# Transposes of an adaptive FFN kernel moved from the DMA queue to TensorE, and the queue reordered

## The chip, the cores and the metric

The kernel runs on one core of one Trainium2 chip. The metric is the device time of one execution in microseconds (us). Before the change it is 73.77 us, the median of three runs (73.26 to 75.43).

## What is computed

x has 2 x 1024 rows of 256 values. Each batch has its own 256x256 matrix, made from 30 ranks, and the result goes through a two-layer network with quantised weights and activations:

```
U = (mu @ W_dec + b_dec).reshape(B, 257, 30)
param = einsum('bik,kj->bij', U, V)                  # V: 30 x 256
y = einsum('bsd,bde->bse', x, param[:, :-1]) + param[:, -1][:, None]
quant_act(v): scale = 127 / max(|v| over the row), then round(v * scale) / scale
quant_weight(w): s = mean(|w|), then clip(round(w / s), -1, 1) * s
h = gelu(quant_act(y) @ quant_weight(w1).T)          # 1024 wide
out = x + quant_act(h) @ quant_weight(w2).T
```

## The kernel before

The 2048 rows are 16 tiles of 128 rows, and two tiles are a pair (0 to 7). A tile goes through these steps. z is the product of x with U (30 wide), made for four tiles at once (`product_z`); y is z times V, made for a pair (`product_y`, line 427). VectorE takes the maxima of y and their reciprocals; ScalarE rounds y by adding a large constant (`quantise_y`, line 573), so that the integer stands in the low 16 bits of an fp32 word. The quantised y has to be transposed before the first product (`product_1`, line 445), whose result ScalarE turns into h by a gelu (line 595). VectorE takes the maxima of h for a pair at once (line 698), GpSimd quantises a tile of h into fp16 with an offset of 1152 added (`quantise_h`, line 366), h is transposed, and the second product (`product_2`, line 462) gives a tile of the output. The offset is taken out by one more product per tile with the row sums of w2 (line 472; the sums are made by `offset_sums`). VectorE scales the result and adds x (`output`, line 740), and SyncE stores a pair.

There are two ways to transpose. For pairs 0 and 1 of y TensorE transposes the low halves and VectorE copies them out of PSUM (`transpose_yq` in the TensorE block, `copy_yqt`, line 691). From pair 2 on GpSimd narrows y to bf16 (`narrow_y`, line 338) and SyncE issues a DMA transpose (line 260); the h of tiles 0 to 13 go by DMA transpose too (line 267). The h of the last two tiles are transposed by TensorE in halves (line 485) and copied out by ScalarE and VectorE (lines 631, 638, 793, 797). Of tile 15 VectorE quantises one half (line 788) and ScalarE the other (line 634).

The order on each engine is written out by hand, and each engine runs its list in order. TensorE's main loop (lines 544 to 550) runs, for p from 3, the first products of pair p, y of pair p + 2 between them, and the second products of pair p - 3. VectorE's (line 770) runs the maxima of h of pair p, an output, the maxima of y of pair p + 3, the scales of both, an output. GpSimd's (line 375) runs tile 2p of h, the small product for the scales, the narrowing of pair p + 3, tile 2p + 1. SyncE's list after the loads is

```
transpose_yq(AHEAD - 1)
for p in range(PAIRS):
    transpose_hq(2 * p)
    if p < Y_PAIRS: transpose_yq(p + AHEAD)
    transpose_hq(2 * p + 1)
    if p >= LAG // 2: store(2 * p - LAG, 2 * p - LAG + 2)
```

with AHEAD = 3, PAIRS = 7, Y_PAIRS = 5 and LAG = 6. The transposed h have six buffers, the quantised h four (a tile waits until the one four before it has been transposed), the h three pairs. Seven products of zeros, `keep_warm(7, ps_o)` (line 537), stand before the product of tile 4.

Of the kernel before, what the change touches and what calls it, by code (L numbers as in the profile page):

```python
# [6 lines left out]
FP16 = mybir.dt.float16  # L7
# [21 lines left out]
def adaln_ffn(nc, x, x_tr, small, w_dec, w1_tr, w2_tr, out):  # L29
# [23 lines left out]
    SINGLE = 2 * PAIRS  # L53

# [4 lines left out]
    with ctx:  # L59
# [79 lines left out]
        def blocks(bank, n, dt=BF16):  # L139
# [11 lines left out]
        ps_yqt = [blocks(ps_o, DC), blocks(ps_z, DC), blocks(ps_o, 2 * DC)]  # L151
# [5 lines left out]
        ps_hqt = {NT - 2: [blocks(ps_y[:, half, :], HC // 2, FP16) for half in range(2)],  # L157
                  NT - 1: [blocks(ps_h[0][:, half, :], HC // 2, FP16) for half in range(2)]}
# [64 lines left out]
        hqt14_done = sem("tile14_hqt_half_done")  # L223
        hqt14_copied = [sem(f"tile14_hqt_copied{n}") for n in range(2)]
        last_hq = [sem(f"last_hq_ready{n}") for n in range(2)]
        last_hqt = sem("last_hqt_half_done")
        last_hqt_copied = [sem(f"last_hqt_copied{n}") for n in range(2)]
# [6 lines left out]
        def yqt_count(p):  # L234

            return 16 * (p // 2)
# [11 lines left out]
        def _(sp):  # L248
# [9 lines left out]
            def transpose_yq(p):  # L258
                sp.wait_ge(yqh_ready, p - 1)
                sp.dma_start_transpose(yq_t[:, p, :, :, :].rearrange("p t c q -> p (t c) q"),  # L260
                                       yq_h[p % 2][:, :, :].rearrange("p t c -> p (t c)")).then_inc(yqt_landed[p % 2], 16)
# [45 lines left out]
        def _(pool):  # L307
# [26 lines left out]
            def narrow_y(p):  # L334
                pool.wait_ge(yq_ready, 2 * p + 2)
                if p >= 4:
# [45 lines left out]
            for n in range(SINGLE, NT):  # L382
                scale_h(n)

        @block.tensor
        def _(pe):
            def keep_warm(n, bank=ps_idle):
                for _ in range(n):
                    nc.tensor.matmul(bank, warm_h[:, 0:P], warm_h[:, :], start=True, stop=True)  # L389
# [17 lines left out]
            def offset_sums():  # L407
                for n in range(2):
# [28 lines left out]
            def transpose_yq(n):  # L437

                pe.wait_ge(yq_ready, (1, 2, 4)[n])
                i0, i1 = ((0, 1), (1, 2), (0, 2))[n]  # L440
                for c in range(DC * i0, DC * i1):
                    last = nc.tensor.transpose(ps_yqt[n][:, c - DC * i0, :], yq_low[n // 2][:, c * P:(c + 1) * P], ident_h[:, :])
                last.then_inc(yqt_done, 1)

            def product_1(n):
# [3 lines left out]
                elif n >= 4 and n % 2 == 0:  # L449
# [12 lines left out]
            def product_2(n):  # L462
# [9 lines left out]
                nc.tensor.matmul(o_of[n], offsets[:, :], w2_off[:, :], start=True, stop=False)  # L472
                if n < NT - 2:
                    pe.wait_ge(hqt_landed[k], 16 * (n // LAG + 1))
                for t in range(HC):
                    if n >= NT - 2 and t % (HC // 2) == 0:
                        pe.wait_ge((hqt14_copied, last_hqt_copied)[n - NT + 2][t // (HC // 2)], 1)
                    last = nc.tensor.matmul(o_of[n], hq_t[k][:, t, :], w2_t[:, t, :], start=False, stop=(t == HC - 1))  # L478
                last.then_inc(mm2_done, 1)

            def transpose_hq(n, half):

                for t in range(HC // 2):
                    c = half * HC // 2 + t
                    last = nc.tensor.transpose(ps_hqt[n][half][:, t, :], hq_h[n % NB][:, c * P:(c + 1) * P], ident_f[:, :])
                last.then_inc((hqt14_done, last_hqt)[n - NT + 2], 1)
# [64 lines left out]
            product_2(NT - 6)  # L551
            product_2(NT - 5)
            pe.wait_ge(hq_ready, NT - 1)
            for half in range(2):
                transpose_hq(NT - 2, half)
            pe.wait_ge(last_hq[0], 1)
# [289 lines left out]
```

## Time and profile before

| | |
|---|---|
| median of three runs | 73.77 us (73.26 to 75.43) |
| the profiled execution | 73.63 us, its span 71.8 us |
| busy, share of the span | TensorE 85%, VectorE 64%, ScalarE 46%, GpSimd 41% |
| HBM read / written | 10.47 MB / 2.10 MB |
| chain of waits, by engine | GpSimd 23%, DMA 19%, TensorE 19%, issue 13%, VectorE 9%, SyncE 8% |

The span is the time from the program's first instruction to its last; the execution's time has something more around it. Busy time counts an engine's own instructions; an engine can be idle and still be the one that the others wait for. In the views PE is TensorE, PEld its weight loads, DVE VectorE, ACT ScalarE, POOL GpSimd and SPq what SyncE issues. The loads end at about 27 us, and the change begins behind them.

### The profile page before, as it was taken

The numbers are of one execution on the slowest core, as the hardware profiler recorded it, in microseconds if no ns is written. First come the engines' busy times: TensorE is split into PE (matmuls) and PEld (weight loads), VectorE is DVE, ScalarE is ACT, GpSimd is POOL, SyncE is SP. The second block draws the span as 40 slices with busy tenths as digits, with TensorE's granted clock in tenths as the row PEclk, the third lists the DMA queues.
The fourth block names the chain that finished last, engine by engine and source line by source line (L and its number), as shares of the span: only waits on it lengthen the run. The fifth ranks groups of instructions, "written<-read, shape, count | busy, mean of one in ns | idle before, by whom it ended". The sixth has DMA issues, their size and how long they took to land.

```text
span 71.8 us, 1271 instructions
## 1 busy us (share of the span) xinstructions
PE 60.8 (85%) x452; PEld 31.6 (44%) x452; DVE 45.9 (64%) x92; ACT 33.3 (46%) x47; POOL 29.5 (41%) x48
## 2 busy tenths in 40 slices
PE   2999999988986999959909999999994698889930
PEld 1315232223323534414603664847662266669820
DVE  2002437644367848999585589798988907998440
ACT  3406009200382979947843766947592074044100
POOL 5500000000001088989596276593969484520000
PEclk9999999999999999999999999999999999999999
DMA  0899999999999995030969979658894699999352
GB/s 7 229 383 415 422 413 410 410 387 409 413 433 415 420 415 246 14 73 10 73 145 176 189 136 187 127 110 170 171 200 100 133 265 175 275 187 365 117 219 73
DMA packets 22086, 17.10 MB, mean 238 GB/s; under 512 B 18496, under 2 KB 18880, under 8 KB 21696
## 3 DMA queue, kind: packets, MB, share of 16 engines
q1 hardware_dynamic: 21936, 16.78, 81.7%
q10 hardware_dynamic: 144, 0.24, 1.6%
q8 instruction: 3, 0.05, 0.4%
q14 instruction: 3, 0.02, 0.1%
HBM read 10.47 MB, written 2.10 MB: 175 GB/s over the span
## 4 chain that ended last, share of the span: by engine, by line
POOL 23%; DMA 19%; PE 19%; issue 13%; DVE 9%; SPq 8%; ACT 4%; POOLq 0%; ACTq 0%
POOL hq_h L366 16%; DMA w_dec_all<-in_w_dec_dram 16%; PE ps_h L457 5%; SPq L250 5%; POOL yq_h L338 4%; PE ps_o L478 4%; DMA yq_t<-yq_h 4%; DVE h_max L716 3%; POOL w_t L351 3%; PE ps_z L478 2%; PE ps_z L422 2%; DVE o_sb L740 2%; ACT w_dec_all L595 2%; ACT y_q L584 1%; ACT w_r L571 1%
## 5 line engine op out<-in xcount | busy, mean ns | idle before, releaser
L366 POOL TENSOR_SCALAR hq_h<-w_dec_all,pair_rcp 128x1024 f16<-128x1024 f32 x14 | 15.7, 1119 | 7.8 <-DVE pair_rcp L712 7.2
L457 PE MATMUL ps_h<-w_t,yq_t 128*128 128x512 bf16 x64 | 15.8, 380 | 3.2 <-DMA yq_t<-yq_h 3.2
L698 DVE TENSOR_REDUCE pair_max<-w_dec_all 128x2 f32<-128x2048 f32 x7 | 15.9, 2273 | 0.0
L595 ACT ACTIVATE w_dec_all<-ps_h,pair_c 128x1024 f32<-128x1024 f32 x10 | 10.9, 1112 | 10.2 <-PE ps_h L457 10.2
L389 PE MATMUL ps_h<-warm_h 128*128 128x512 bf16 x39 | 13.3, 462 | 1.3 <-POOL warm_h L308 1.3
L457 PEld LDWEIGHTS ps_h<-w_t,yq_t 128*128 128x128 bf16 x64 | 5.6, 98 | 10.5 <-DMA yq_t<-yq_h 4.3
L478 PE MATMUL ps_z<-w_t,hq_t 128*128 128x256 f16 x64 | 8.3, 273 | 1.0 <-DMA hq_t<-hq_h 1.0
L324 POOL TENSOR_TENSOR c<-y_inv,s 128x2 f32<-128x2 f32 x3 | 0.6, 194 | 20.3 <-DVE y_inv L686 20.3
L478 PE MATMUL ps_o<-w_t,hq_t 128*128 128x256 f16 x64 | 8.3, 273 | 0.5 <-DMA hq_t<-hq_h 0.5
L389 PEld LDWEIGHTS ps_h<-warm_h 128*128 128x128 bf16 x39 | 3.8, 119 | 7.9 <-issue 6.1
L478 PEld LDWEIGHTS ps_z<-w_t,hq_t 128*128 128x128 f16 x64 | 6.1, 98 | 2.1 <-DMA hq_t<-hq_h 1.4
L478 PEld LDWEIGHTS ps_o<-w_t,hq_t 128*128 128x128 f16 x64 | 6.1, 98 | 2.0 <-DMA hq_t<-hq_h 0.8
L567 ACT ACTIVATE w_abs<-w_sb 128x1024 f32<-128x1024 f32 (+1 forms) x3 | 2.7, 914 | 9.1 <-DMA w_sb<-in_w_tr_dram 9.0
L595 ACT ACTIVATE w_dec_all<-ps_h,c 128x1024 f32<-128x1024 f32 x6 | 6.5, 1114 | 0.9 <-PE ps_h L457 0.9
L740 DVE SCALAR_TENSOR_TENSOR o_sb<-ps_o,pair_c,x_sb 128x256 f32<-128x256 f32 x7 | 3.4, 483 | 4.4 <-PE ps_o L478 4.4
L646 DVE TENSOR_REDUCE w_sum<-w_sb 128x1 f32<-128x1024 f32 (+1 forms) x2 | 1.9, 948 | 5.4 <-DMA w_sb<-in_w_tr_dram 5.4
L571 ACT ACTIVATE w_r<-w_sb,s_rcp 128x1024 int16<-128x1024 f32 x3 | 3.3, 1141 | 4.1 <-DVE s_rcp L656 4.1
L434 PE MATMUL ps_y<-small_sb,z_t 30*128 30x256 f32 x28 | 4.9, 425 | 0.2 <-DVE z_t L677 0.2
L584 ACT ACTIVATE y_q<-ps_y,pair_rcp 128x256 f32<-128x256 f32 x10 | 4.2, 471 | 1.0 <-DVE pair_rcp L712 1.0
L703 DVE TENSOR_REDUCE pair_max<-ps_y 128x2 f32<-128x512 f32 x5 | 3.4, 685 | 1.4 <-PE ps_y L434 1.4
L338 POOL TENSOR_SCALAR yq_h<-y_q 128x512 bf16<-128x512 f32 x6 | 3.7, 617 | 0.7 <-ACT y_q L584 0.7
L740 DVE SCALAR_TENSOR_TENSOR o_sb<-ps_z,pair_c,x_sb 128x256 f32<-128x256 f32 x7 | 3.3, 477 | 0.7 <-PE ps_z L478 0.7
(88 smaller groups left out, 68.3 us busy)
## 6 DMA issues: line engine op xcount, KB each, us to landing
w_sb<-in_w_tr_dram SPq DMA_DIRECT2D x4, 512.0 KB, 8.8
x_sb<-in_x_dram SPq DMA_DIRECT2D x2, 1024.0 KB, 18.9
out_dram<-o_sb SPq DMA_DIRECT2D x7, 256.0 KB, 2.7
w_dec_all<-in_w_dec_dram SPq DMA_DIRECT2D x3, 512.0 KB, 7.5
w_dec_all<-in_w_dec_dram SPq DMA_DIRECT2D x3, 448.0 KB, 8.2
x_t<-in_x_tr_dram SPq DMA_DIRECT2D x1, 1024.0 KB, 16.5
w_dec_all<-in_w_dec_dram SPq DMA_DIRECT2D x1, 576.0 KB, 10.5
x_t<-in_x_tr_dram SPq DMA_DIRECT2D x2, 256.0 KB, 11.0
```

Source lines behind the costliest of these rows:

```text
L250: sp.dma_start(w_dec_all[:, starts[n]:starts[n + 1]], w_dec[:, starts[n]:starts[n + 1]]).then_inc(s_wdec[n], 16)
L338: pool.tensor_scalar(yq_h[p % 2][:, :, :].rearrange("p t c -> p (t c)"), y_q[p % 2][:, :, :].rearrange("p t c -> p (t c)"), 1.0, -MAGIC, A ...
L366: pool.tensor_scalar(hq_h[n % NB][:, :], h_tile(n), scale, H_OFFSET, ALU.mult, ALU.add).then_inc(hq_ready, 1)
L389: nc.tensor.matmul(bank, warm_h[:, 0:P], warm_h[:, :], start=True, stop=True)
L434: last = nc.tensor.matmul(y_of[p][:, i, 0:D], z_t[p // 2][r:r + K, :], v_sb[r:r + K, :], start=True, stop=True)
L457: last = nc.tensor.matmul(ps_h[k][:, half, :], yq_t[:, p, n % 2, c, :], w1_t[:, c, half * HALF:(half + 1) * HALF], start=(c == 0), stop=(c ...
L478: last = nc.tensor.matmul(o_of[n], hq_t[k][:, t, :], w2_t[:, t, :], start=False, stop=(t == HC - 1))
L571: nc.scalar.activation(dst, src, ACT.Copy, scale=scale).then_inc(done, 1)
L584: nc.scalar.activation(y_q[p % 2][:, i, :], y_of[p][:, i, 0:D], ACT.Copy, bias=MAGIC, scale=scale).then_inc(yq_ready, 1)
L595: nc.scalar.activation(h_tile(n), ps_h[n % 2][:, :, :].rearrange("p a n -> p (a n)"), ACT.Gelu, scale=c1_of(n)).then_inc(gelu_done, 1)
L698: nc.vector.tensor_reduce(pair_max[:, p, 2:4], h_pair[p % NH], AXX, ALU.max, apply_absolute_value=True).then_inc(pair_max_ready, 1)
L740: nc.vector.scalar_tensor_tensor(o_sb[p % NO][:, i, :], o_of[n], c2_of(n), x_sb[:, b, t, :], ALU.mult, ALU.add).then_inc(out_ready, 1)
```

## The change

Three things change. Pairs 2 and 3 of y are transposed by TensorE like pairs 0 and 1, but ScalarE copies them out; GpSimd narrows only pairs 4 to 7. The seven products of zeros go, and the row sums of w2 are made behind the product of tile 6. SyncE's list has the store first, then y, then both tiles of h. The h of tiles 12 and 13 join those of 14 and 15: TensorE transposes them in halves, and ScalarE and VectorE copy them out and take the offset off in the copy, so these four tiles have no product with the row sums. GpSimd takes over ScalarE's half of tile 15.

```
 SyncE
-            transpose_yq(AHEAD - 1)
             for p in range(PAIRS):
-                transpose_hq(2 * p)
-                if p < Y_PAIRS:
-                    transpose_yq(p + AHEAD)
-                transpose_hq(2 * p + 1)
                 if p >= LAG // 2:
                     store(2 * p - LAG, 2 * p - LAG + 2)
+                if 1 <= p < Y_PAIRS:
+                    transpose_yq(p + AHEAD)
+                if 2 * p < LATE:                      # LATE = NT - 4
+                    transpose_hq(2 * p)
+                    transpose_hq(2 * p + 1)
 GpSimd
-            narrow_y(AHEAD - 1)
...
-                if p < Y_PAIRS:
+                if 1 <= p < Y_PAIRS:
                     narrow_y(p + AHEAD)
...
-            for n in range(SINGLE, NT):
-                scale_h(n)
+            scale_h(NT - 2)
+            pool.wait_ge(h_rcp_ready, NT - SINGLE)
+            pool.wait_ge(hqt_landed[(NT - 1 - NB) % LAG], 16 * ((NT - 1 - NB) // LAG + 1))
+            pool.tensor_scalar(hq_h[(NT - 1) % NB][:, HALF:], h_tile(NT - 1)[:, HALF:], h_rcp[:, NT - 1:NT], H_OFFSET,
+                               ALU.mult, ALU.add).then_inc(last_hq[1], 1)
+            scale_h(NT - 1)
 TensorE
             product_z(2)
+            transpose_yq(3)
             product_y(3)
-            keep_warm(7, ps_o[:, :])
             product_1(4)
             product_1(5)
+            transpose_yq(4)
             product_y(4)
-            offset_sums()
             pe.wait_ge(z_copied, 3)
             product_z(3)
             for p in range(LAG // 2, NP):
                 product_1(2 * p)
+                if p == LAG // 2:
+                    offset_sums()
...
-            product_2(NT - 6)
-            product_2(NT - 5)
-            (transposes of tiles 14 and 15 between the second products 10 to 15)
+            for n in range(LATE, NT):
+                for half in range(2):
+                    transpose_hq(n, half)
+                product_2(n - 2)
+            product_2(NT - 2)
+            product_2(NT - 1)
 ScalarE
             for p in range(AHEAD, NP):
                 gelu(2 * p - 4)
-                gelu(2 * p - 3)
-                if p == AHEAD + 1:
+                if p - 1 < 4:
+                    copy_yqt(p - 1)
+                if p == AHEAD + 2:
                     ...                                # the copy of the row sums
+                gelu(2 * p - 3)
                 quantise_y(p)
...
+            def copy_yqt(p):
+                act.wait_ge(yqt_done, p + 2)
+                nc.scalar.activation(yq_t[:, p, ...], ps_yqt[p + 1].bitcast(I16), ACT.Copy,
+                                     bias=-OFFSET).then_inc(yqt_copied, 1)
+            for n, half in ((LATE, 0), (LATE, 1), (LATE + 1, 0), (LATE + 1, 1), (LATE + 2, 0), (LATE + 3, 1)):
+                act.wait_ge(late_hqt, 2 * (n - LATE) + half + 1)
+                act.wait_ge(mm2_done, n - LAG + 1)
+                part = slice(half * HC // 2, (half + 1) * HC // 2)
+                nc.scalar.activation(hq_t[n % LAG][:, part, :], ps_hqt[n][half], ACT.Copy,
+                                     bias=-H_OFFSET).then_inc(late_copied[n][half], 1)
 VectorE, after its half of tile 15
             output(NT - 6)
             output(NT - 5)
+            copy_late(NT - 2, 1)                       # a tensor_scalar that adds -H_OFFSET
+            copy_late(NT - 1, 0)
             for n in range(NT - 4, NT):
                 output(n)
```

The late tiles' transposes go to the banks of y and of the first products, each with a wait for its last reader.

## Rows read from the trace of the kernel before

**Rows 1.** The page, costliest groups: count | busy us, mean ns | idle us before, releaser.
```profile
L366 POOL TENSOR_SCALAR hq_h<-w_dec_all,pair_rcp 128x1024 f16<-128x1024 f32 x14 | 15.7, 1119 | 7.8 <-DVE pair_rcp L712 7.2
...
L698 DVE TENSOR_REDUCE pair_max<-w_dec_all 128x2 f32<-128x2048 f32 x7 | 15.9, 2273 | 0.0
...
L324 POOL TENSOR_TENSOR c<-y_inv,s 128x2 f32<-128x2 f32 x3 | 0.6, 194 | 20.3 <-DVE y_inv L686 20.3
...
L584 ACT ACTIVATE y_q<-ps_y,pair_rcp 128x256 f32<-128x256 f32 x10 | 4.2, 471 | 1.0 <-DVE pair_rcp L712 1.0
L703 DVE TENSOR_REDUCE pair_max<-ps_y 128x2 f32<-128x512 f32 x5 | 3.4, 685 | 1.4 <-PE ps_y L434 1.4
```

**Rows 2.** The page: granted clock in 40 slices; an instruction queue's packets.
```profile
PEclk9999999999999999999999999999999999999999
...
q8 instruction: 3, 0.05, 0.4%
```

**Rows 3.** The chain of waits around 54 us: start, length, what.
```profile
54.19 2.58 DMA yq_t<-yq_h
```

**Rows 4.** The timeline, 28 to 34 us: start, length, what [idle before <- releaser].
```profile
28.62 2.12 ACT L595 ACTIVATE w_dec_all<-ps_h,c 128x1024 f32<-128x1024 f32 x2
28.82 0.62 POOL L338 TENSOR_SCALAR yq_h<-y_q 128x512 bf16<-128x512 f32 x1 [0.40 <-ACT y_q L584]
...
29.41 2.04 POOL L351 TENSOR_SCALAR w_t<-w_r 128x1024 f16<-128x1024 int16 x2
...
29.51 1.69 PE L389 MATMUL ps_o<-warm_h 128*128 128x512 bf16 x7
...
30.61 0.87 DVE L709 TENSOR_SCALAR pair_inv<-pair_max 128x4 f32<-128x4 f32 x1
...
31.84 2.27 DVE L698 TENSOR_REDUCE pair_max<-w_dec_all 128x2 f32<-128x2048 f32 x1
```

**Rows 5.** The timeline, 35 to 47 us.
```profile
35.31 0.17 DVE L709 TENSOR_SCALAR pair_inv<-pair_max 128x4 f32<-128x4 f32 x1
...
37.87 1.04 PE L457 MATMUL ps_h<-w_t,yq_t 128*128 128x512 bf16 x4 [1.78 <-DMA yq_t<-yq_h]
...
42.31 1.03 PE L457 MATMUL ps_h<-w_t,yq_t 128*128 128x512 bf16 x4
...
43.27 0.70 PE L434 MATMUL ps_y<-small_sb,z_t 30*128 30x256 f32 x4
...
46.74 1.03 PE L457 MATMUL ps_h<-w_t,yq_t 128*128 128x512 bf16 x4
```

**Rows 6.** SyncE's timeline: a store's issue.
```profile
50.81 0.58 SPq L274 DMA_DIRECT2D out_dram<-o_sb  x1
```

**Rows 7.** By tile, h and y: issues in ns and landing in us, min/median/max.
```profile
L267 SPq DMA_TRANSPOSE hq_t<-hq_h x14: 1233/1302/2653, 32.9 to 62.3; - x14
...
DMA to landing us min/median/max: 3.1/3.4/5.6
...
L260 SPq DMA_TRANSPOSE yq_t<-yq_h x6: 1262/1278/2325, 29.5 to 54.2; - x6
...
DMA to landing us min/median/max: 2.5/2.5/3.6
```

**Rows 8.** The timeline, 55 to 70 us.
```profile
55.14 1.05 PE L478 MATMUL ps_z<-w_t,hq_t 128*128 128x256 f16 x8 [0.99 <-DMA hq_t<-hq_h]
...
56.82 1.90 PE L457 MATMUL ps_h<-w_t,yq_t 128*128 128x512 bf16 x8 [0.63 <-DMA yq_t<-yq_h]
...
63.35 0.61 PE L485 MATMUL ps_y<-ident_f,hq_h 128*128 128x128 f16 x8
...
63.77 0.60 ACT L631 ACTIVATE hq_t<-ps_y 128x512 f16<-128x512 f16 x1 [3.76 <-PE ps_y L485]
...
64.75 1.04 PE L478 MATMUL ps_o<-w_t,hq_t 128*128 128x256 f16 x8
...
68.99 0.48 DVE L740 SCALAR_TENSOR_TENSOR o_sb<-ps_z,c,x_sb 128x256 f32<-128x256 f32 x1 [0.50 <-PE ps_z L478]
```

More of the change, by code:

```diff
@@ L222, in adaln_ffn @@
         out_ready = sem("out_ready")
-        hqt14_done = sem("tile14_hqt_half_done")
-        hqt14_copied = [sem(f"tile14_hqt_copied{n}") for n in range(2)]
+        late_hqt = sem("late_hqt_half_done")
+        late_copied = {n: [sem(f"late_hqt{n}_copied{half}") for half in range(2)] for n in range(LATE, NT)}
         last_hq = [sem(f"last_hq_ready{n}") for n in range(2)]
-        last_hqt = sem("last_hqt_half_done")
-        last_hqt_copied = [sem(f"last_hqt_copied{n}") for n in range(2)]
         store_done = [sem(f"store_done{k}") for k in range(NO)]
@@ L437, in transpose_yq @@
             def transpose_yq(n):
-                pe.wait_ge(yq_ready, (1, 2, 4)[n])
-                i0, i1 = ((0, 1), (1, 2), (0, 2))[n]
+                p, i0, i1 = YQT_PARTS[n]
+                pe.wait_ge(yq_ready, 2 * p + i1)
+                if n > 2:
+                    pe.wait_ge(yqt_copied, n)
                 for c in range(DC * i0, DC * i1):
-                    last = nc.tensor.transpose(ps_yqt[n][:, c - DC * i0, :], yq_low[n // 2][:, c * P:(c + 1) * P], ident_h[:, :])
+                    last = nc.tensor.transpose(ps_yqt[n][:, c - DC * i0, :], yq_low[p % 2][:, c * P:(c + 1) * P], ident_h[:, :])
                 last.then_inc(yqt_done, 1)
@@ L448, in product_1 @@
                     pe.wait_ge(yqt_copied, n + 1)
-                elif n >= 4 and n % 2 == 0:
+                elif n in (4, 6):
+                    pe.wait_ge(yqt_copied, p + 2)
+                elif n >= 8 and n % 2 == 0:
                     pe.wait_ge(yqt_landed[p % 2], yqt_count(p))
@@ L471, in product_2 @@
                     pe.wait_ge(out_ready, n - 1)
-                nc.tensor.matmul(o_of[n], offsets[:, :], w2_off[:, :], start=True, stop=False)
-                if n < NT - 2:
+                if n < LATE:
+                    nc.tensor.matmul(o_of[n], offsets[:, :], w2_off[:, :], start=True, stop=False)
                     pe.wait_ge(hqt_landed[k], 16 * (n // LAG + 1))
                 for t in range(HC):
-                    if n >= NT - 2 and t % (HC // 2) == 0:
-                        pe.wait_ge((hqt14_copied, last_hqt_copied)[n - NT + 2][t // (HC // 2)], 1)
-                    last = nc.tensor.matmul(o_of[n], hq_t[k][:, t, :], w2_t[:, t, :], start=False, stop=(t == HC - 1))
+                    if n >= LATE and t % (HC // 2) == 0:
+                        pe.wait_ge(late_copied[n][t // (HC // 2)], 1)
+                    last = nc.tensor.matmul(o_of[n], hq_t[k][:, t, :], w2_t[:, t, :], start=(n >= LATE and t == 0), stop=(t == HC - 1))
                 last.then_inc(mm2_done, 1)
             def transpose_hq(n, half):
+                if n < NT - 1:
+                    pe.wait_ge(hq_ready, n + 1)
+                else:
+                    pe.wait_ge(last_hq[half], 1)
+                if n == LATE:
+                    pe.wait_ge(yq_ready, NT)
+                elif n == LATE + 2:
+                    pe.wait_ge(late_copied[LATE][half], 1)
+                else:
+                    pe.wait_ge(gelu_done, NT - 1 if n == LATE + 1 else NT)
                 for t in range(HC // 2):
@@ L485, in transpose_hq @@
                     last = nc.tensor.transpose(ps_hqt[n][half][:, t, :], hq_h[n % NB][:, c * P:(c + 1) * P], ident_f[:, :])
-                last.then_inc((hqt14_done, last_hqt)[n - NT + 2], 1)
+                last.then_inc(late_hqt, 1)
             pe.wait_ge(s_warmh, 1)
@@ L550, in _ @@
                 product_2(2 * p - LAG + 1)
-            product_2(NT - 6)
-            product_2(NT - 5)
[L553 to L556, printed above, removed]
-            transpose_hq(NT - 1, 0)
-            product_2(NT - 4)
-            pe.wait_ge(last_hq[1], 1)
-            transpose_hq(NT - 1, 1)
-            for n in range(NT - 3, NT):
-                product_2(n)
+            for n in range(LATE, NT):
[4 more added lines that the diff above has]
+            product_2(NT - 1)
         @block.scalar
@@ L741, in output, with copy_late @@
                                                ALU.mult, ALU.add).then_inc(out_ready, 1)
+            def copy_late(n, half):
+                dve.wait_ge(late_hqt, 2 * (n - LATE) + half + 1)
+                dve.wait_ge(mm2_done, n - LAG + 1)
+                part = slice(half * HC // 2, (half + 1) * HC // 2)
+                nc.vector.tensor_scalar(hq_t[n % LAG][:, part, :], ps_hqt[n][half], -H_OFFSET, None,
+                                        ALU.add).then_inc(late_copied[n][half], 1)
             nc.vector.memset(ps_z[:, :], 0.0).then_inc(s_psz, 1)
```

42 lines of the change are left out of this document (15 added, 27 removed).

## The prediction

> **What bounds the kernel now.** I began with the page. Its costliest groups [rows 1] show three streams that are nearly level over the second half of the span: VectorE with seven maxima of h of 2.27 us, GpSimd with fourteen quantisations of 1.12 us, and ScalarE with its gelus. None is full by itself, so the question is which wait ends last. The granted clock is 9 tenths or more in every slice [rows 2], the 2.4 GHz level, so the clock takes nothing now.
>
> The timeline of the middle [rows 5] gives the rhythm: the product of tile 8 starts at 42.31 and that of tile 10 at 46.74, 4.43 us for a pair in which TensorE never waits. VectorE's work in the same pair is 2.27 + 0.68 [rows 1] + two outputs of 0.48 [rows 8] + 0.4 for a scaling, a reciprocal of its size and the hops between them [rows 5], that is 4.3 at most. So here TensorE is the bound with VectorE close behind.
>
> The lost time is at three places, and each waits for a transposed tile. Tile 6's first product waits 1.78 us for pair 3 of y [rows 5]. Tile 7's second product waits 0.99 us for its h, and right behind it tile 14's first product 0.63 us for pair 7 of y [rows 8]. The chain of waits runs through that last one: its transfer takes 2.58 us from its issue at 54.19 [rows 3]. Two rows say why it was late. SyncE needs about 1.3 us to issue any transpose, and two issues, one of h and one of y, took 2.65 and 2.33 us instead [rows 7]; one transfer of h took 5.6 us to land against a median of 3.4 [rows 7]. I call these two events holds. One delayed pair 3, the other tile 7's h and pair 7. Without the second one tile 14 could have started where TensorE was free: 51.17, where tile 12's product ran (4.43 behind tile 10's 46.74), plus two first products of 0.87 and two second ones of 0.98, 54.9 instead of 56.82.
>
> From tile 14 to the last output at 68.99 + 0.48 = 69.47 the kernel is one ladder of VectorE and TensorE steps of 12.65 us.
>
> **Part 1, pairs 2 and 3 of y through TensorE.** Removed from GpSimd: the narrowing of pair 2, 0.62 us, which runs just ahead of the two clips of w2, 2.04 us, that end at 31.45 [rows 4]. VectorE's tiny scaling began at 30.61 and took 0.87 us, against 0.17 in another pair [rows 5]: it ended when the clips ended. With the clips 0.4 to 0.6 earlier (they then wait for GpSimd's own scale of y) they end near 30.5, before VectorE asks. The reciprocal of pair 0 comes at about 31.1, 0.6 earlier. The Trainium skill (GPSIMD Engine Reference, Specifications) says that GpSimd shares its SBUF interfaces with VectorE when that is in a two-port mode; the row agrees, and it is a warning for part 3.
>
> Added to ScalarE: two copies of 128x512 out of PSUM. The nearest row is the copy of half a tile of h, same shape, 0.60 us [rows 8]; a gelu of twice the columns, 1.06, bounds it above [rows 4], and 0.47 for half the columns bounds it below (line 584) [rows 1]. I take 0.6. The first stands before the gelu of tile 3, so that one ends at 31.3, not 30.74, and the maximum of pair 1, which began at 31.84 because of the scaling, begins at 31.4. Added to TensorE: eight transposes of 128 columns, eight of the same shape in fp16 take 0.61 [rows 8]; they stand where seven warming products of 1.69 us stood [rows 4], so they cost nothing; without that cover they would be 0.3 each.
>
> Now step by step. VectorE: 31.4 + 2.27 + 0.68 + 0.4 gives the reciprocals of pair 1 at 34.8. GpSimd then quantises (1.12), multiplies its scales (0.2 by the small product of line 324) [rows 1] and narrows pair 4 (0.62) [rows 4], 0.1 with the hops: 36.85. Its transfer, 2.5 us [rows 7], lands at 39.4. TensorE: the gelu of tile 4 ends at 33.2, ScalarE's second copy at 33.8, so tile 6's product starts at 34.0 instead of 37.87. Behind its 0.87 (eight in 1.90 are two tiles) come the row sums of w2 (eight of 256 columns, 1.0) [rows 8], y (0.70) [rows 5], tile 7 (0.87) and two second products (1.96), which with the hops fill up to 39.4. Both sides meet there: tile 8 starts at 39.4 instead of 42.31, **2.9 us earlier**. A copy of 1.06 instead of 0.6 would take up to 0.5 of this back.
>
> **Part 2, the order of the queue.** Two h transposes of each pair now stand behind its y, and a store of 0.58 [rows 6] ahead of it. The store asks for an output that VectorE makes before the reciprocals that this y needs, so it adds its issue and no wait. The h that are pushed back have three pairs until they are read. TensorE keeps its 4.43: tile 12 at 48.3, tile 14 possible at 48.3 + 3.7 = 52.0. But SyncE becomes the tighter queue: from pair 4's issue at 36.85 to pair 7's there are three rounds of 1.28 + 2 x 1.30 + gaps of 0.15 = 4.03 and two stores of 0.65, so pair 7 is issued at 50.2 and lands at 52.7. That is 56.82 - 52.7 = **4.1 earlier if nothing holds the queue**.
>
> The two holds were not made by this order. What I can see beside them is that the page counts three packets of 16 KB in an instruction queue which take 0.4% of sixteen engines' span, 1.5 us each [rows 2], and a hold is 1.05 to 1.35 us longer than a normal issue [rows 7]. My guess, which no view of this profile shows, is that these packets refill TensorE's program at fixed places of it and that a transpose in flight then is held. TensorE's program is hardly longer ahead of tile 13 (14 instructions of the warming products go, 16 of the transposes come). Then the first falls on h transposes with slack, and the second near 49 to 51, where transposes of h 7 and y 7 follow each other without a gap. I take it to come again, at 1.2 us: tile 14 at 53.9, **2.9 earlier**. The Trainium skill, Runtime: NRT & Kernel Launch, Instruction fetch mechanics, calls the crossing of a 16 KiB boundary mostly hidden; by that nothing is held in the new order, which is the first rival.
>
> **Part 3, the last four tiles.** Added to TensorE: sixteen transposes, 2 x 0.61 = 1.22 [rows 8]; removed: four products with the offsets, of 256 columns and so 0.11 apiece by the eight in 1.04, 0.44 in all. Added to ScalarE: four more copies, 2.4 us, in a stretch where it waited 3.76 us before its one; its half of tile 15's quantisation goes to GpSimd (0.62, by the narrowing of the same shape [rows 4]). The ladder from tile 14: VectorE's output 8, two maxima, two scales, output 9, its half of tile 15 and output 10 are the same steps as before and lead to tile 12's second product 7.9 us behind tile 14's start (64.75 less 56.82) [rows 8]. Then 0.87 + transposes 0.53 + 3 x 0.87 + drain 0.17 + output 0.48 = 4.66, 12.5 in all against 12.65: **0.15 less**. The extra transposes of tiles 12 and 13 fall into the wait for output 10. If that cover is gone they cost 1.2 - 0.44 = 0.8. GpSimd and VectorE now quantise their halves of tile 15 side by side; if they exclude each other as at 30.61, one of them is 0.5 to 0.6 late. Tile 15's transposes come some 0.8 later than that, so I take 0, and keep 0.6 for the range.
>
> Nothing in the tail now needs h transposes 12 to 15 from the queue, which frees 5.2 us of SyncE (4 x 1.30); that was not on the chain, and I count it at zero. The last stores are the same.
>
> **Sum.** The profiled execution took 73.63 us with a span of 71.8; it lies 0.14 under the median of 73.77. 2.9 + 0.15 = 3.1 off gives 70.5 from the profiled execution and 70.7 from the median; I take **70.5**.
>
> **Rivals.**
> No hold on the path: 4.1 + 0.15 off, **69.4**. For it: the hold needs a transpose just then, and there are six fewer of them. Against: the queue is denser around pair 7.
> The queue or ScalarE takes more back: issue times of 1.4 instead of 1.3 over nine issues ahead of pair 7 (0.9), or copies at their upper bound, with a hold: **71.7**. Against: SyncE's median is firm.
> The tail becomes the bound: TensorE's added 0.8, the halves of tile 15 in turn 0.6, and the start of tile 14 held twice (1.2): 70.5 + 2.6 = **73.1**, no difference. It decides if output 10 no longer is what tile 12's product waits for.
> Slower: TensorE's clock. The warming products go, and TensorE waits from 29.9 to 30.3 for ScalarE's copy and 0.1 to 0.2 for the gelu of tile 3 at 31.3. If the granted clock fell to 1.2 GHz there, eight products that take 1.90 [rows 8] would take 3.8; TensorE has some 9 us of work from 30.3 up to tile 8 at 39.4, so it is slower than before by over 2% once the low level lasts over 4.6 us: **79** if it lasts all of it. Against: a wait of 1.78 us in rows 5 did not lower it, and the new ones are shorter.
> That the change does not do what it says is no separate case: pair 3 of y and the h of tiles 12 to 15 no longer pass the queue at all.
>
> **Chances.** Forecast 0.45, no hold 0.25, queue or copies 0.17, tail 0.10, clock 0.03. A measurement can tell 2% from no change, that is 72.3 and below or 75.2 and above. So faster 0.88 (a part of the third case lies above 72.3, a part of the tail below), same 0.10, slower 0.02. The range goes from 68.9 (no hold, and issues at their shortest, 1.23 to 1.26, nine times 0.05) to 72.1 (the third case with half a microsecond of tail).
>
> **What would show it.** The profile after should have tile 6's product near 34.0, tile 8's at 39.4, tile 14's between 52.7 and 54; VectorE's scaling of pair 0 at 0.17 us; a period of 4.4 between; SyncE issuing with no gap from pair 4 on; 12.5 us from tile 14 to the end. The prediction is wrong if tile 14 still waits for y by more than 2 us, if ScalarE's gelus start late behind its copies, or if the tail is longer than 13 us.

## The result, and the profile after

| | median, us | lowest to highest | executions |
|---|---|---|---|
| before | 74.60 | 73.26 to 76.03 | 4 |
| changed | 71.15 | 70.77 to 72.01 | 4 |

The ratio of changed to before is 0.968, 95% interval 0.958 to 0.979: faster, by 3.2%. A second measurement of the same two kernels (the first run below) gave 0.969 (0.961 to 0.976). The ratios leave disturbed executions out and the medians don't (before's 75.43 and 76.03 raise its median), so the two medians are further apart, 4.6%, than the ratio says. The profiled execution took 70.77 us with a span of 68.9, against 73.63 and 71.8: 2.86 us less.

The core's granted clock, the packets of the instruction queue and two groups of the page, for [rows 1, 2]. A quantisation of h costs what it did (1.12 us), and so does a maximum (2.28 us), so the gain is in waits and in the products of zeros that filled one.

```profile
core 0: 68.9 us, clock 1.000
q8 instruction: 3, 0.05, 0.3%
L367 POOL TENSOR_SCALAR hq_h<-w_dec_all,pair_rcp 128x1024 f16<-128x1024 f32 x14 | 15.7, 1122 | 8.4 <-DVE pair_rcp L729 6.1
L486 PE MATMUL ps_o<-w_t,hq_t 128*128 128x256 f16 x64 | 8.3, 273 | 2.1 <-DMA hq_t<-hq_h 1.8
```

The timeline from 29 to 40 us, which answers [rows 4] and the head of [rows 5]: start, length, what, idle before. The scaling of pair 0 (line 726) takes 0.17 where it took 0.87. Tile 6's product starts 0.17 ahead of the line at 34.08 (one of its four records is missing), and pair 4 of y is issued at 36.84.

```profile
29.78 0.61 ACT L614 ACTIVATE yq_t<-ps_o 128x512 bf16<-128x512 int16 x1
30.77 0.17 DVE L726 TENSOR_SCALAR pair_inv<-pair_max 128x4 f32<-128x4 f32 x1
...
31.43 2.29 DVE L715 TENSOR_REDUCE pair_max<-w_dec_all 128x2 f32<-128x2048 f32 x1
...
34.08 0.81 PE L465 MATMUL ps_h<-w_t,yq_t 128*128 128x512 bf16 x3 [0.16 <-issue]
...
36.84 1.19 SPq L261 DMA_TRANSPOSE yq_t<-yq_h  x1
...
39.28 1.04 PE L465 MATMUL ps_h<-w_t,yq_t 128*128 128x512 bf16 x4
```

The same view from 44 to 55 us, which answers [rows 5, 6] and the first two lines of [rows 8]. SyncE issues with no gap. Its h transposes issued at 46.82 land late; tile 6's second product (51.85) waits 1.62 us for them, GpSimd (51.96) waits 1.64 us for the same transfer, because the buffer it wants to write is still being read, and tile 14's product waits for pair 7 of y. Its first record is missing: it began at 54.06, so of the 0.40 us in its line only some 0.2 are a wait (0.15 in the profile of the swap below, where no record is missing).

```profile
44.85 0.58 SPq L275 DMA_DIRECT2D out_dram<-o_sb  x1
45.48 1.23 SPq L261 DMA_TRANSPOSE yq_t<-yq_h  x1
46.82 2.62 SPq L268 DMA_TRANSPOSE hq_t<-hq_h  x2
...
50.12 1.72 SPq L261 DMA_TRANSPOSE yq_t<-yq_h  x1
51.85 1.05 PE L486 MATMUL ps_o<-w_t,hq_t 128*128 128x256 f16 x8 [1.62 <-DMA hq_t<-hq_h]
51.96 1.12 POOL L367 TENSOR_SCALAR hq_h<-w_dec_all,pair_rcp 128x1024 f16<-128x1024 f32 x1 [1.64 <-DMA hq_t<-hq_h]
54.28 1.67 PE L465 MATMUL ps_h<-w_t,yq_t 128*128 128x512 bf16 x7 [0.40 <-DMA yq_t<-yq_h]
```

By tile, h and then y, as in [rows 7]: issues in ns, landing in us, each as minimum, median and maximum.

```profile
L268 SPq DMA_TRANSPOSE hq_t<-hq_h x12: 1237/1297/2307, 32.4 to 56.7; - x12
DMA to landing us min/median/max: 3.1/3.3/5.0
L261 SPq DMA_TRANSPOSE yq_t<-yq_h x4: 1190/1254/1724, 36.8 to 50.1; - x4
DMA to landing us min/median/max: 2.4/2.6/3.9
```

The chain that ended last, from 46 us to tile 10's second product; its columns are start, length, what. [Rows 3] had a transfer of y there. Now the chain has two of h. The first holds the buffer that GpSimd wants for tile 10 (51.96). The chain then goes on through tile 11's quantisation (53.45), which ends as SyncE comes free, but that is a coincidence.

```profile
46.82 4.98 DMA hq_t<-hq_h
51.96 0.71 POOL hq_h L367
...
53.45 1.12 POOL hq_h L367
54.62 0.57 SPq L275
55.28 3.31 DMA hq_t<-hq_h
58.64 1.05 PE ps_o L486 x8
```

Tile 10's h was ready at 51.96 + 1.12 = 53.08 and still was not issued before 55.28. SyncE's own timeline shows why: behind pair 7 (50.12) it issues the h of tiles 8 and 9, a store, and then tile 10's h, without a gap. So it is the full queue that sets tile 10's product, not GpSimd.

```profile
51.94 2.63 SPq L268 DMA_TRANSPOSE hq_t<-hq_h  x2
54.62 0.57 SPq L275 DMA_DIRECT2D out_dram<-o_sb  x1
55.28 2.66 SPq L268 DMA_TRANSPOSE hq_t<-hq_h  x2
```

The tail, against the rest of [rows 8]. From tile 14's start (about 54.06) to the end of the last output (66.49) it takes 12.43 us; it took 12.65.

```profile
60.92 0.49 DVE L812 TENSOR_SCALAR hq_h<-w_dec_all,h_rcp 128x512 f16<-128x512 f32 x1
60.99 0.98 POOL L385 TENSOR_SCALAR hq_h<-w_dec_all,h_rcp 128x512 f16<-128x512 f32 x1 [0.52 <-DVE h_rcp L741]
61.33 0.48 DVE L757 SCALAR_TENSOR_TENSOR o_sb<-ps_o,pair_c,x_sb 128x256 f32<-128x256 f32 x1
61.86 1.05 PE L486 MATMUL ps_o<-w_t,hq_t 128*128 128x256 f16 x8 [0.30 <-DVE o_sb L757]
...
66.01 0.48 DVE L757 SCALAR_TENSOR_TENSOR o_sb<-ps_z,c,x_sb 128x256 f32<-128x256 f32 x1 [0.39 <-PE ps_z L486]
```

### The profile page after: what moved, and what is told of

It is laid out like the page before. It is cut to its first block, busy times and chain, and to the rows that moved or that the text cites. A ratio compares the mean times of both kernels' runs of the same rounds, so it can differ in the third digit from the quotient of the medians.

```text
span 68.9 us, 1306 instructions
## 1 busy us (share of the span) xinstructions
PE 58.7 (85%) x459; PEld 31.7 (46%) x465; DVE 45.1 (65%) x92; ACT 35.6 (52%) x52; POOL 29.4 (43%) x47
## 4 chain that ended last, share of the span: by engine, by line
DMA 28%; PE 18%; DVE 14%; SPq 12%; POOL 9%; ACT 7%; issue 7%; POOLq 0%; DVEq 0%
DMA w_dec_all<-in_w_dec_dram 16%; DMA hq_t<-hq_h 12%; POOL hq_h L367 7%; DVE pair_max L715 7%; SPq L251 5%; PE ps_o L486 4%; PE ps_z L486 4%; ACT w_dec_all L609 4%; PE ps_h L465 2%; PE ps_z L427 2%; SPq L261 2%; DVE pair_max L720 2%; SPq L275 2%; ACT y_q L598 1%; SPq L268 1%
## 5 line engine op out<-in xcount | busy, mean ns | idle before, releaser
L465 PE MATMUL ps_h<-w_t,yq_t 128*128 128x512 bf16 x60 | 15.1, 380 | 1.1 <-ACT yq_t L614 0.5
L393 PE MATMUL ps_h<-warm_h 128*128 128x512 bf16 x37 | 12.4, 450 | 1.5 <-POOL warm_h L309 1.3
L348 POOL TENSOR_SCALAR w_r<-w_sb,s_rcp 128x1024 int16<-128x1024 f32 x1 | 2.8, 2848 | 1.9 <-DVE s_rcp L673 1.9
```

The costliest lines, as they stand in the source:

```text
L393: nc.tensor.matmul(ps_idle, warm_h[:, 0:P], warm_h[:, :], start=True, stop=True)
L465: last = nc.tensor.matmul(ps_h[k][:, half, :], yq_t[:, p, n % 2, c, :], w1_t[:, c, half * HALF:(half + 1) * HALF], start=(c == 0), stop=(c ...
```

## The experiments

**The changed kernel again**, unaltered.

> The changed kernel unaltered, for a narrower interval. Theory (the start is 2.9 us earlier, the hold comes again, the tail costs 0.1): profiled execution again 70.8 +- 0.3 and a ratio to before of 0.96. If the gain in the profiles (73.63 to 70.77) was luck of one execution of before, the ratio is 0.97 or more.

Median 71.59 of 6 (70.53 to 72.15), ratio 0.969 (0.961 to 0.976). The profiled execution took 70.53, 3.1 us less than before's: tile 8 at 39.06, tile 14 at 53.77, the wait of tile 6's second product 1.65. The other five took 71.06, 71.15, 72.02, 72.06 and 72.15. Of the last three, two have a span of 70.3 to 70.4 instead of 69.1 at a clock of 1.000, and one has an ordinary span of 69.2 and 1 us more outside it. So one kernel comes in kinds over 1 us apart, and its profile showed the shortest. The three shorter executions average 70.91, 3.9% under 73.82, the mean of before's executions that the ratio counts; all six average 71.50, 3.1% under. The expectation gave 0.96 for a true gain of the size seen in the profiles and 0.97 or more for luck of one execution of before; 0.969 lies next to the second.

**The three parts, one at a time.** Part 1 alone, built on before:

```diff
-            return 16 * (p // 2)
+            return 16 * (p // 2 - 1)
...
-            transpose_yq(AHEAD - 1)        # SyncE
-            narrow_y(AHEAD - 1)            # GpSimd
-            keep_warm(7, ps_o[:, :])       # TensorE
+            transpose_yq(3)                # TensorE
...
+            transpose_yq(4)
+                copy_yqt(p - 1)            # ScalarE, for p - 1 < 4
```

> The kernel before with part 1 alone: pairs 2 and 3 of y through TensorE and ScalarE's copies, the queue in its old order and tiles 12 and 13 by DMA. Theory: all of the 2.9 us up to tile 8 comes from this part (tile 8's product at 39.3 to 39.7), and the second hold comes again: 70.8 to 71.5. Rival (the order of the queue carries the gain, y of pair 4 waits behind h): tile 8's product at 40.6 or later, time 72 or more.

Median 71.41 of 4 (71.22 to 72.40), ratio 0.965 (0.961 to 0.970). That is the whole gain of the change, within the interval. Tile 8's product starts at 40.38, though, and not at the 39.3 to 39.7 that were expected: in the old order pair 4 of y stands behind an h. In TensorE's timeline y is late at tile 8 and at tile 14:

```profile
40.38 1.04 PE L460 MATMUL ps_h<-w_t,yq_t 128*128 128x512 bf16 x4 [0.60 <-DMA yq_t<-yq_h]
54.66 1.90 PE L460 MATMUL ps_h<-w_t,yq_t 128*128 128x512 bf16 x8 [1.56 <-DMA yq_t<-yq_h]
```

Part 2 alone, built on before:

```diff
-                transpose_hq(2 * p)
+                if p >= LAG // 2:
+                    store(2 * p - LAG, 2 * p - LAG + 2)
                 if p < Y_PAIRS:
                     transpose_yq(p)
+                transpose_hq(2 * p)
                 transpose_hq(2 * p + 1)
-                if p >= LAG // 2:
-                    store(2 * p - LAG, 2 * p - LAG + 2)
```

> The kernel before with part 2 alone: in SyncE's list the store first, then y, then both tiles of h. Theory: pair 3 of y is no longer behind tile 0's h, so its issue goes before h, but it can only be issued once GpSimd has narrowed it; tile 0's h then waits for it. Tile 6's product a little earlier if the first hold falls on h (36.5 to 37.9), pair 7 still held by the block near 50: 72.3 to 74, ratio 0.98 to 1.00. Rival (the order is what counts): as good as part 1, ratio 0.965.

Median 73.85 of 10 (73.20 to 74.31), ratio 1.004 (0.999 to 1.008): nothing. Tile 14 starts at 55.32 instead of 56.82, yet TensorE waits later, for h: at 61.20 tile 10's second product waits 1.67 us. With y first, the last h that pass the queue are what is late (TensorE's timeline).

```profile
55.32 1.90 PE L457 MATMUL ps_h<-w_t,yq_t 128*128 128x512 bf16 x8
...
61.20 1.05 PE L478 MATMUL ps_o<-w_t,hq_t 128*128 128x256 f16 x8 [1.67 <-DMA hq_t<-hq_h]
```

Part 3 alone, built on before (the first line of TensorE's new tail; the queue's h transposes stop at tile 11):

```diff
+    LATE = NT - 4
...
+            for n in range(LATE, NT):
+                for half in range(2):
+                    transpose_hq(n, half)
+                product_2(n - 2)
```

> The kernel before with part 3 alone: tiles 12 and 13 of h through TensorE, their offsets taken off in the copies, tile 15's second half quantised by GpSimd. Theory: the ladder from tile 14's product to the last output stays 12.3 to 12.7 us, so the time is 0.1 to 0.3 below before, ratio 0.995 to 1.00. Rival (the end was held up by h transposes 12 and 13 in the queue): 1 us or more off, ratio 0.985 or less. Rival (the added transposes and copies cost): 0.8 more, ratio 1.01.

Median 73.66 of 10 (73.03 to 76.46), ratio 1.002 (0.998 to 1.005): nothing. Its ladder from tile 14 (56.52) to the end of the last output (68.96) is 12.44 us, 0.2 less than before's.

**The changed kernel with the old order of the queue**, so parts 1 and 3.

```diff
-                if p >= LAG // 2:
-                    store(2 * p - LAG, 2 * p - LAG + 2)
+                if 2 * p < LATE:
+                    transpose_hq(2 * p)
```

> The changed kernel with the queue's old order (h, y, h, then the store). Theory: each y is issued about 1.3 us later and each first h 1.5 us earlier; tile 8's product at 40.0 to 40.4 instead of 39.3, tile 7's second product no longer waits 1.6 us for tile 6's h, but tile 14's waits for pair 7 as it did with part 1 alone: time within 0.5 us of the changed kernel, ratio to before 0.96 to 0.975. Rival (the new order carries a part of the gain): 72.3 or more, ratio 0.98 or more.

Median 71.75 of 4 (71.21 to 72.17), ratio 0.976 (0.968 to 0.984). With the order in, it was 0.969 (0.961 to 0.976): the point values differ by 0.7%, the intervals overlap, so the gain of the order is not shown in time. Nor is one of part 3: this kernel is no faster than part 1 alone (0.965, 0.961 to 0.970). In the profile the order trades waits: 1.57 us for y at tile 14 and 0.52 at tile 8, against 1.62 for h and some 0.2 for y. Here no transfer of y is held (by tile, this kernel's issues and landings of y; compare 1724 ns and 3.9 us above).

```profile
L261 SPq DMA_TRANSPOSE yq_t<-yq_h x4: 1266/1274/1284, 37.8 to 52.0; - x4
DMA to landing us min/median/max: 2.5/2.5/2.7
```

**Do the 16 KB packets hold the transposes?** If they refill TensorE's program, more TensorE instructions early bring them earlier, and the holds with them, at the same work. So products of 512 columns became four of 128 or eight of 64. In the changed kernel, 36 instructions more (18 products and their weight loads) at the first warming products:

```diff
-            keep_warm(9)
+            keep_warm(3)
+            keep_warm_short(6)     # 4 x 6 products of 128 columns
```

> The changed kernel with six of the nine first warming products (512 columns) cut into four of 128 columns each: the same busy time, 36 more TensorE instructions ahead of everything. Theory 'instruction block': the 16 KB packets come at fixed places of TensorE's program, so they move 36 instructions earlier: the second to about 29.6 us, where no transpose is in flight (both first h issues then 1.3 us, the first h lands 3.2 us behind its issue and not 3.6), the third from 49.4 to about 46.8, so tile 6's h (5.0 us to land) is held less or not, and some issue near 47 may be long instead. Tile 14's product 0.4 to 1.5 us earlier than 54.1, time 69.3 to 70.5. Rival 'queue order' (the hold comes from a store among transposes or from the queue being full): long issue and 5 us landing stay at the same transfer near 50, time 70.8 to 71.2.

Median 72.70 of 4 (71.63 to 73.54), ratio 0.976 (0.967 to 0.986). The third packet came at 47.20 instead of 49.35, and the hold moved with it: it is pair 6 of y now (4.6 us to land) and the h issued before it, so that tile 12 waits and tile 14 doesn't (the landing of y by tile, then TensorE's timeline).

```profile
DMA to landing us min/median/max: 2.4/2.5/4.6
```
```profile
49.80 1.05 PE L490 MATMUL ps_z<-w_t,hq_t 128*128 128x256 f16 x8 [1.04 <-DMA hq_t<-hq_h]
51.47 1.90 PE L469 MATMUL ps_h<-w_t,yq_t 128*128 128x512 bf16 x8 [0.63 <-DMA yq_t<-yq_h]
```

The second packet did not come earlier as expected: 34.84, against 33.22 and 34.94 in the two profiles of the changed kernel, and tile 0's h took 4.3 us to land. And the expected gain (69.3 to 70.5) was missed: the median is 1.1 us above the repeat's and the profiled span 1.6 us (70.2 against 68.6). The first packet, now at 16.84 by the packet records and not 20.99, met a plain load: the chain of waits has a transfer of x_t of 12.59 us that the changed kernel's has not. It landed at 19.17 instead of 17.86, and what is behind it is late (the product of tile 4 at 31.76 instead of the repeat's 30.20; from there to tile 14 23.41 us, against 23.57).

```profile
6.59 12.59 DMA x_t<-in_x_tr_dram
```

In before, 54 instructions more at the same place:

```diff
-            keep_warm(9)
+            keep_warm_short(9)
```

> The kernel before with all nine first warming products cut into four of 128 columns: 54 more TensorE instructions. Theory 'instruction block': the second packet moves from 34.0 to about 28.5, so pair 3 of y is not held: tile 6's product at 36.4 to 36.6 instead of 37.87; the third moves to about 47, where it holds an h with slack instead of tile 7's h and pair 7. Time 2 to 3 us less than before, 70.8 to 72. Rival 'queue order': both holds stay at the same transfers, time as before, 73.6.

Median 74.63 of 10 (73.24 to 75.23), ratio 0.998 (0.994 to 1.003). That is nothing, where 2 to 3 us were expected. The late transfers of the middle did move, from tile 7's h and pair 7 to an h and pair 6, which tile 12 waits for in TensorE's timeline; tile 14 waits for nothing. But the first packet (16.92) met the load of x_t here too (landed at 19.23 instead of 17.70), so tile 4's product came at 33.55 instead of 32.01; and the second came at 35.24, not near 28.5, and held tile 0's h, whose issue of 2.52 us stands ahead of pair 3, so tile 6 waited 2.00 us instead of 1.78.

```profile
54.43 1.90 PE L461 MATMUL ps_h<-w_t,yq_t 128*128 128x512 bf16 x8 [1.33 <-DMA yq_t<-yq_h]
```

In the changed kernel, 56 instructions more (28 products and their weight loads), placed behind the first packet, so that it stays where it was and only the later ones move:

```diff
-            keep_warm(4)
+            keep_warm_short(4)     # 8 x 4 products of 64 columns
```

> The changed kernel with the four warming products behind the first y (512 columns each) cut into eight of 64 columns each: 56 more TensorE instructions, put behind the first 16 KB packet and ahead of the second. Theory 'instruction block': the loads are as in the changed kernel (tile 4's product at 30.2 to 30.8), the second packet comes near 30, before any transpose, so tile 0's h lands 3.3 us behind its issue instead of 3.6 to 4.9, and the third comes near 45.5 instead of 49.2, where the transfers issued from 43.5 to 46.8 are held instead of tile 6's h and pair 7. Time 70.3 to 71.3. Rival 'queue order': the transfers of tile 6 and pair 7 are held as before, 5.0 and 3.9 us to land.

Median 70.84 of 4 (70.76 to 71.17), ratio 0.965 (0.960 to 0.970), which overlaps the 0.969 (0.961 to 0.976) of the changed kernel. The second packet came at 28.45, before any transpose was in flight, and the first pair of h landed unheld, in 3.4 us; the third came at 45.84 and held pair 6 of y, 4.3 us to land. Again the stall went to tile 12, in TensorE's timeline (tile 14 waited 0.30):

```profile
48.60 1.05 PE L490 MATMUL ps_z<-w_t,hq_t 128*128 128x256 f16 x8 [0.78 <-DMA hq_t<-hq_h]
50.22 1.90 PE L469 MATMUL ps_h<-w_t,yq_t 128*128 128x512 bf16 x8 [0.57 <-DMA yq_t<-yq_h]
```

**The tail: output 10 ahead of VectorE's half of tile 15**, in the changed kernel.

```diff
+            output(NT - 6)
             ...                    # VectorE's half of tile 15
-            output(NT - 6)
```

> The changed kernel with VectorE's output 10 ahead of its half of tile 15 instead of behind it. Theory (tile 12's second product is held by output 10, and tile 15's transposes come later): that product starts 0.4 to 0.5 us sooner behind tile 14's than the 7.8 us of the changed kernel, the ladder from tile 14 to the end is 11.9 to 12.1 us instead of 12.4, time 0.3 to 0.5 lower. Rival (TensorE's own work sets the tail): no change, or tile 15 late by the same amount.

Median 70.79 of 4 (70.16 to 71.35), ratio 0.961 (0.955 to 0.967). The interval overlaps that of the changed kernel (0.961 to 0.976), so in time the gain is likely and not shown. In the profile it is: tile 12's second product starts at 61.36, not 61.86, and the ladder is 11.99 us (53.99 to 65.98) instead of 12.43. GpSimd's half takes 0.69 here, where VectorE's work beside it begins later, against 0.98. The timeline from 60.9 us:

```profile
60.92 0.69 POOL L385 TENSOR_SCALAR hq_h<-w_dec_all,h_rcp 128x512 f16<-128x512 f32 x1 [0.49 <-DVE h_rcp L741]
61.17 0.73 DVE L813 TENSOR_SCALAR hq_h<-w_dec_all,h_rcp 128x512 f16<-128x512 f32 x1
61.36 1.04 PE L486 MATMUL ps_o<-w_t,hq_t 128*128 128x256 f16 x8
```

**The first two stores from ScalarE's queue**, so that SyncE has them no longer; with the swap.

```diff
-                if p >= LAG // 2:
+                if p > 4:
...
+                if p >= 6:
+                    act_store(p - 6)
```

> The kernel of c1_swap with the first two stores issued by ScalarE behind its roundings of pairs 6 and 7, not by SyncE. Theory (SyncE's issues of 4.66 us a pair are over TensorE's 4.43, and the h behind y is late): tile 6's h is issued 0.6 us sooner and lands before the third 16 KB packet, so its wait of 1.6 us goes; pair 7 is held by the packet still and lands near 53; tile 14's product 0.8 to 1.2 us sooner, time 69.3 to 70. Rival (the hold alone sets tile 14): no more than 0.6 sooner, the issue that was saved.

Median 71.61 of 4 (70.90 to 72.61), ratio 0.967 (0.961 to 0.972), no better than the swap alone. SyncE has two stores less to issue, but nothing came of it: the h of tiles 4 and 5, in flight beside the first store, landed in 4.4 and 4.7 us instead of 3.4 and 3.3 (the swap's profile), tile 5's issue took 2.04 us instead of 1.33, and tile 6's h was issued at 47.19, where the swap has 46.81. Over all h the median is 3.8 us, not 3.3. TensorE waits for h three times (0.15 us at 46.80, and the two lines below the landings of h):

```profile
DMA to landing us min/median/max: 3.1/3.8/5.6
```
```profile
48.38 1.05 PE L486 MATMUL ps_z<-w_t,hq_t 128*128 128x256 f16 x8 [0.43 <-DMA hq_t<-hq_h]
52.88 1.05 PE L486 MATMUL ps_o<-w_t,hq_t 128*128 128x256 f16 x8 [1.59 <-DMA hq_t<-hq_h]
```

**The same with half the shift**, 28 instructions more.

```diff
-            keep_warm(4)
+            keep_warm(2)
+            keep_warm_short(2)
```

> The kernel of c2_stores_act with two of the four warming products behind the first y cut into eight of 64 columns: 28 more TensorE instructions. Theory 'instruction block': the third packet comes near 47.3 instead of 49.2 and holds tile 6's or 7's h by 1.2 us at most, before pair 7 is issued; pair 7 lands 2.5 us behind its issue, tile 14's product near 52 to 52.7, time 68.9 to 69.8, the fastest of all. Rival: any place of the packet costs the same as the queue is full, time as c2_stores_act.

Median 71.06 of 6 (70.63 to 72.13), ratio 0.966 (0.961 to 0.972). The third packet did not come earlier (50.79 against 50.60) and the largest wait for h stayed, 1.73 us. This one tells nothing of the shift.

**The swap with the whole shift.**

```diff
-            keep_warm(4)
+            keep_warm_short(4)
+            output(NT - 6)         # moved ahead, as in the swap
```

> The changed kernel with output 10 ahead of VectorE's half of tile 15 (c1_swap) and with the 56 more TensorE instructions of b4_a_lateshift56: the two edits that looked best, together. Theory: their effects are in different stages and add, 0.45 us in the ladder behind tile 14 and a second packet that falls where nothing is held; 70.2 to 70.6, and the executions lie within 0.6 us of each other, ratio to before 0.955 to 0.962. Rival (the spread of the changed kernel's executions, 70.5 to 72.2, has nothing to do with the packets): spread of 1.3 us or more, median 70.8 or more.

Median 70.71 of 6 (70.36 to 71.00), ratio 0.961 (0.958 to 0.964): the lowest median of all, and the narrowest interval. The swap alone has the same ratio, so what the shift adds is not shown; and the interval still overlaps that of the changed kernel (0.961 to 0.976). Tile 14 starts at 53.36, 0.7 earlier than after, and the end is only 0.4 earlier (66.09 against 66.49): tile 10's second product waits 0.68 us for its h and starts at 58.71, where it started at 58.64. SyncE issued that h at 55.22 (55.28 after): its queue was as full, as the held issue is now pair 6's (1.76 us) instead of pair 7's (1.72).

**The clock: five warming products behind the first y left out** of the changed kernel (they were there before the change as well).

```diff
-            keep_warm(4)
...
-            keep_warm(1)
```

> The changed kernel without five warming products of 512 columns behind the first y (four and one): ten TensorE instructions fewer ahead of the second packet, which in the changed kernel came at 33.2 in one execution and at 34.9 in another. Theory (the packet at its later place nearly reaches pair 4 of y, issued at 36.8; a little later it holds it): in some executions tile 8's product is late by 0.5 to 1 us, median 71.4 to 72.2, spread 1.3 us or more. Rival 'neutral': the products only filled a wait, 71.1 and the same spread.

This was meant to bring the second packet later, and the clock hid what that did. Median 72.75 of 6 (70.87 to 73.69), against 73.75 for before beside it; no ratio, as the six fall apart: one at a mean clock of 1.000 took 70.87, the other five, at 0.972 to 0.976, 72.37 to 73.69. TensorE sat idle from 20.6 to 22.1, and between 24 and 25 us the clock fell. The changed kernel with its products showed 0.999 to 1.000 in all ten of its executions; but two of the eleven of before beside this run showed 0.977 with the products in, so they are no guarantee. The page's row of granted clock, and two of the products by line: four of 512 columns take 1.91 and, 2.5 us on, eight take 1.90, so the first ran at the 1.2 GHz level.

```profile
PEclk9999999999999856999999999999999999999999
```
```profile
22.09 0.27 PE L448 MATMUL ps_o<-ident_h,y_q 128*128 128x128 bf16 x2 [1.51 <-ACT y_q L596]
...
25.79 1.91 PE L465 MATMUL ps_h<-w_t,yq_t 128*128 128x512 bf16 x4
...
28.27 1.90 PE L465 MATMUL ps_h<-w_t,yq_t 128*128 128x512 bf16 x8
```

## Why the prediction was right in part 1 and the tail, and wrong on the h and the size

**Part 1: right, step by step.** ScalarE's copy 0.61 (0.6), the scaling 0.17 (0.17), the reciprocal 31.16 (31.1), the maximum 31.43 (31.4), pair 4 issued 36.84 (36.85), tile 6 at 33.9 (34.0), tile 8 at 39.28 (39.4). Part 1 alone also has the whole gain. So the way of pairs 2 and 3 through TensorE is the cause; how much of it is GpSimd's free time and how much the queue was not taken apart.

**Part 2: the time of tile 14 right, one reason wrong.** Two pairs take 8.94 us (2 x 4.43 forecast), tile 12 starts at 48.22 (48.3), pair 7 is issued at 50.12 (50.2), is held and lands at 54.01, and tile 14 starts at 54.06 (53.9). The step that failed is "The h that are pushed back have three pairs until they are read", by which their wait was counted at nothing. Tile 6's h was issued at 46.82, where the old order had it at 44.57. At the median of 3.3 us it would have landed at 50.1, and TensorE wanted it at 50.23: the slack was a tenth of a microsecond, and then the packet held it. It came 1.62 us late for TensorE (1.65 in the repeat) and 1.64 late for the buffer that GpSimd wanted. TensorE was then free for tile 14 only some 0.2 us before it started, not at the 52.0 of the forecast. So the time of tile 14 is right for the reason given, the landing of pair 7, and a second wait as long stood beside it unseen. The order takes a wait from y and gives it to h, and alone it is worth nothing (1.004).

**The hold: the guess is borne out.** The trace's packet records put the three packets at 20.96, 33.98 and 52.21 us before and at 20.99, 33.22 and 49.35 after, each of the last two inside a late landing. With instructions added ahead of it the third came earlier each time but in the run with the half shift (47.20, 45.84 and 45.58 in the changed kernel, 49.82 in before), and the late transfers moved with it: from tile 7's h and pair 7 to pair 6 in before; from pair 7 to pair 6 in the changed kernel, in all three. The second is looser: it came at 33.22 and 34.94 in two profiles of the same kernel, and tile 0's h landed in 3.6 and 4.9 us; only the 56 instructions behind the first packet brought it clearly earlier (28.45 and 30.90). So "fixed places" is borne out for the third packet only. The first rival (no hold) fell: a transpose in flight there is held in the new order as in the old. The Trainium skill, Runtime: NRT & Kernel Launch, Instruction fetch mechanics, calls the crossing of a 16 KiB boundary mostly hidden. For TensorE itself that may be so; this trace shows its cost on another transfer, 1.3 to 2.0 us over the median of its kind (pair 7 or 6 of y in 3.9, 4.6 and 4.3 us against 2.6).

**Part 3: 12.43 us against 12.5.** (The steps as listed, 7.93 + 4.66, make 12.6.) The copies and transposes are hidden as said. GpSimd's half took 0.98 instead of 0.62, and the slack covered it. What I had not seen is that VectorE's half stood ahead of output 10 and cost 0.4 there, which the swap shows. I also took tile 14 to be the only start of this ladder. The full queue sets a second floor at the same place: tile 10's h lands at 58.6. With the swap and the whole shift tile 14 was 0.7 earlier and the product at 58.7 did not move.

**The sum: what failed is that one execution stood for all.** In the profiled executions the terms hold: tile 14 came 2.76 us earlier (2.9 forecast) and the tail took 0.22 less (0.15); 2.86 us were saved in one and 3.1 in the repeat, and I had forecast 3.1. But side by side the ratio is 3.2% off (2.2 to 4.2), not the 4.2% that 3.1 us are of 73.63, and against 70.5 the median was 71.15, then 71.59. "I take it to come again, at 1.2 us" and "I take **70.5**" made one number, read off one execution, of something that differs from execution to execution: the same changed kernel took 70.53 and 72.15, and its shorter kind alone is 3.9% off in the repeat. The sum had no term for the longer kind.

What makes that kind is open. Where the second packet came before any transpose was in flight, ten executions in two kernels stayed within 0.41 and 0.64 us, none with a span over 70; of the 22 executions of the kernels in which nothing was added (the changed one, its repeat, part 1 alone, the old order, the swap) five had one. That speaks for the packets, weakly: the two profiles of the changed kernel have the second packet 1.7 us apart and spans of 68.9 and 68.6. No execution of it with a span of 70.3 was profiled, and the extra microsecond outside the span in others (one in six of the repeat) is unexplained.

**The other rivals.** Queue or copies dearer: issues of 1.25 and 1.30 and copies of 0.61 rule it out, though its 71.7 is near the measured time for another reason (its own terms, 0.9 or 0.5 on 70.5, give 71.4 or 71.0). The tail: no. The clock: it stayed at 1.000, so the seven warming products were indeed not needed; but my reason, that a wait of 1.78 us had not lowered it, carries less than I thought: with five others left out, an idle time of 1.51 us in a stretch of light work went with a lower clock in five executions of six.

## What to carry to other kernels

A queue that is full trades waits when its order changes: ask of each transfer that is pushed back when it is read and when its source buffer is wanted again, and expect a gain only where a transfer leaves the queue. A stall that does not fit the schedule may belong to a place in an engine's instruction stream: add instructions without adding work and see whether it moves. Size a change on several executions; the profiled one may be the shortest kind.

## What the hardware did that I had not expected

- A 16 KB packet of instructions delays a transfer on another queue by more than a microsecond, plain loads included (a load of x_t landed 1.3 us later in the run with 36 instructions more, and 1.5 in the one with 54).
- The issue of a transposing transfer costs SyncE nearly the same for 512 columns (1.25 us) as for 1024 (1.30), so a store, a y and two h fill its queue for 4.64 us (44.85 to 49.49), which is more than TensorE's 4.47 for a pair.
- A store issued from a second queue slows the transposes in flight beside it: tiles 4 and 5 of h landed in 4.4 and 4.7 us instead of 3.4 and 3.3. Whether the same store from SyncE's queue would do so too was not tried.
- GpSimd's quantisation of 128x512 took 0.98 us with VectorE's 0.49 us on the same tile beside it, and 0.69 when VectorE began 0.25 us later and itself took 0.73.
